# A causal mask moved from TensorE to GpSimd in the feed-forward attention of a four-layer kernel

## Reference, cut to what matters

```python
qkv = x @ W_qkv.T                                  # x is layer-normed
k_shared = einsum('bth,bthd->btd', indicator, k)   # one of 16 heads per token
v_shared = einsum('bth,bthd->btd', gating_top1, v)
att = einsum('bhqd,bkd->bhqk', q, k_shared) * (1.0 / sqrt(16))
att = where(tril, att, -inf)
att = softmax(att, axis=-1)
y = einsum('bhqk,bkd->bhqd', att, v_shared)
```

## Time and profile before

| | |
|---|---|
| time before, median of 3 runs | 1210.67 us (1209.03 to 1211.82) |
| the profiled execution: its time | 1211.78 us |
| the profiled execution: its span | 1210.0 us |
| busy: PE, PEld, DVE | 1032.8 us, 801.7 us, 755.6 us |
| busy: ACT, POOL | 523.2 us, 286.1 us |
| first feed-forward layer | about 344 us to 532 us |
| second feed-forward layer | about 1020 us to the end |

### The profile page before, as it was taken

The page is one execution under the profiler, slowest core; times in us unless marked ns, Lnnn a source line. Parts: engine busy times, 40 slices in busy tenths (PEclk is TensorE's granted clock), DMA queues, the critical chain, the costliest instruction groups (busy, mean ns, idle before and its releaser), DMA issues.

```text
span 1210.0 us, 20375 instructions
## 1 busy us (share of the span) xinstructions
PE 1032.8 (85%) x6976; PEld 801.7 (66%) x6976; DVE 755.6 (62%) x2242; ACT 523.2 (43%) x1369; POOL 286.1 (24%) x284
## 2 busy tenths in 40 slices
PE   0689999988758999946798989898998997799997
PEld 0577777776447777625676777676776776677764
DVE  5355666666358888713466656566565664788883
ACT  1114444344402444531256555455555564154545
POOL 4227667667700011000110101111010100000101
PEclk9867887778868999976899999899999998799999
DMA  4443322233023232241000000000000000433330
GB/s 174 71 71 72 68 56 63 59 57 61 1 44 76 59 77 59 47 152 62 1 2 1 2 2 1 1 1 1 1 1 1 1 1 2 87 77 76 85 77 29
DMA packets 56790, 53.71 MB, mean 44 GB/s; under 512 B 6240, under 2 KB 55408, under 8 KB 56560
## 3 DMA queue, kind: packets, MB, share of 16 engines
q1 hardware_dynamic: 56688, 52.41, 18.9%
HBM read 34.30 MB, written 17.30 MB: 43 GB/s over the span
## 4 chain that ended last, share of the span: by engine, by line
PE 69%; DVE 14%; POOL 8%; issue 4%; DMA 3%; ACT 2%; SPq 1%; POOLq 0%; ACTq 0%; DVEq 0%
PE bank L243 20%; PE bank L1529 6%; PE bank L1474 5%; PE bank L1332 4%; PE bank L1462 4%; PE bank L1537 3%; PE bank L1346 3%; PE bank L1329 3%; POOL weights L536 3%; PE bank L1515 2%; PE bank L1316 2%; PE bank L1367 2%; PE bank L348 1%; PE bank L1526 1%; DMA arena<-b_wo 1%
## 5 line engine op out<-in xcount | busy, mean ns | idle before, releaser
L972 DVE TENSOR_REDUCE arena<-bank 128x2 f32<-128x512 f32 (+1 forms) x192 | 129.7, 683 | 32.5 <-PE bank L1332 31.6
L670 ACT ACTIVATE weights<-bank 128x512 f32<-128x512 f32 x144 | 85.7, 596 | 109.1 <-PE bank L1346 108.9
L738 ACT ACTIVATE weights<-bank,neg_max 128x128 f32<-128x128 f32 (+1 forms) x256 | 105.0, 418 | 47.8 <-DVE neg_max L1123 47.7
L1332 PE MATMUL bank<-kf_stack,q_stack 96*128 96x128 f32 (+1 forms) x512 | 113.4, 327 | 0.0
L259 POOL TENSOR_SCALAR var_eps<-mv 128x2 f32<-128x2 f32 x32 | 7.0, 219 | 430.3 <-DVE mv L253 430.3
L536 POOL TENSOR_SCALAR weights<-weights 128x512 f32<-128x512 f32 x64 | 96.4, 1509 | 47.7 <-ACT weights L614 47.4
L1529 PE MATMUL bank<-kbT,arena 128*128 128x128 f32 (+1 forms) x512 | 107.1, 333 | 0.0
L1346 PE MATMUL bank<-q_stack,kf_stack 98*128 98x512 f32 x192 | 97.7, 513 | 0.0
L745 ACT ACTIVATE weights<-bank 128x384 f32<-128x384 f32 x128 | 62.7, 490 | 64.3 <-PE bank L1537 64.1
L1132 DVE TENSOR_SCALAR weights<-weights,inv_sum 128x128 f32<-128x128 f32 (+1 forms) x256 | 85.0, 374 | 4.5
L277 PE MATMUL bank<-cst,xn 128*128 128x128 f32 x128 | 24.0, 319 | 72.3 <-DVE xn L268 70.5
(11 more groups left out here) (214 smaller groups left out, 2724.8 us busy)
## 6 DMA issues: line engine op xcount, KB each, us to landing
q_stack<-scr_q SPq DMA_DIRECT2D x144, 128.0 KB, 3.7
scr_q<-q_hi SPq DMA_DIRECT2D x24, 256.0 KB, 2.3
scr_q<-q_lo SPq DMA_DIRECT2D x24, 256.0 KB, 2.5
ka_stack<-scr_k SPq DMA_DIRECT2D x48, 76.5 KB, 3.2
x_all<-x SPq DMA_DIRECT2D x8, 256.0 KB, 9.1
arena<-b_wqn SPq DMA_DIRECT2D x1, 2048.0 KB, 8.2
arena<-b_wo SPq DMA_DIRECT2D x1, 2048.0 KB, 17.0
out<-x_all SPq DMA_DIRECT2D x8, 256.0 KB, 2.3
```

The lines of the kernel that those rows point to most:

```text
L670: a.activation(pT[(STEPS * b + k) % N_PT], p2[k % 2][:, :], ACT.Exp).then_inc(s["exp"], 1)
L738: last = a.activation(probs[:, h % 4, t * P:t * P + n], ps_s[h % 2][:, t * P:t * P + n], ACT.Exp, bias=neg_max[:, h % 4, t:t + 1], accum_o ...
L972: v.tensor_reduce(into, p1[k % 2][:, :].rearrange("p (h k) -> p h k", h=n), AX.X, ALU.max, negate=True).then_inc(s["maxed"], 1)
L1332: last = mm(o[:, i, :], q_stack[b % 2][0:STK, h + i, t * P:(t + 1) * P], kf_stack[b % 3][0:STK, 0:(t + 1) * P], start=False, stop=i == n - ...
```

## The change

TensorE no longer writes a mask ahead of the second pass's scores. The scores matmul opens its bank itself, and ScalarE takes the exponential of all of them, later keys too. GpSimd then writes zero over the exponentials of later keys in the first 128 queries of each head of the item (two or four heads), in place in `pT`, where position decides: it keeps an element where query minus key (the partition) is at least zero. `attend_f` waits for this, by a new semaphore `causal`, in place of `exp`. On GpSimd's queue `causal(b-1, k)` stands behind `pool_rstd` at k = 3 and ahead of the residual at k = 8. The first pass keeps its mask.

```diff
+            zero = g.to_reg(0.0)
...
             def ffn(s):
+                def causal(b, k):
+                    n = 2 if k % 6 < 4 else 4
+                    part = pT[(STEPS * b + k) % N_PT].rearrange("p (h q) -> p h q", h=n)[:, :, 0:P]
+                    pool.wait_ge(*at(s, "exp", b, k + 1))
+                    g.affine_select(part, part, [[0, n], [1, P]], ALU.is_ge, zero, base=0, channel_multiplier=-1)\
+                        .then_inc(s["causal"], 1)
+
                 for b, k in steps_f():
                     if k == 3 and there(b + 2):
                         pool_rstd(s, b + 2)
+                    if there(b - 1):
+                        causal(b - 1, k)
                     if k == 8 and there(b - 2):
                         residual(s, b - 2, y_flat, at(s, "y", b - 2, 6))
...
-                def turned_mask(out_ap, n):
-                    mm(out_ap, mask_bf[:, :], ident_bf[:, :].unsqueeze(1).to_broadcast([P, n, P]), start=True, stop=False,
-                       skip_group_check=True)
...
                     pe.wait_ge(*at(s, "exp", b, k - 1))
-                    n, kb = (2, 0) if k % 6 < 4 else (4, 1)
-                    o = p2[k % 2][:, :].rearrange("p (h q) -> p h q", h=n)
-                    turned_mask(o[:, :, 0:P], n)
+                    kb = 0 if k % 6 < 4 else 1
                     mm(p2[k % 2][:, :], kf_stack[b % 3][:, kb * P:(kb + 1) * P], item_heads(q_stack[b % 2], k),
-                       start=False, stop=True, skip_group_check=True).then_inc(s["sT_ps"], 1)
+                       start=True, stop=True).then_inc(s["sT_ps"], 1)
...
-                    pe.wait_ge(*at(s, "exp", b, 6 * o + (6 if part == 2 else 4)))
+                    pe.wait_ge(*at(s, "causal", b, 6 * o + (6 if part == 2 else 4)))
```

More of the change, by code:

```diff
@@ L144, in hybrid_layers_kernel @@
         sf = [signals("ffn", "f", **TURNED, q_ps=1, kg_ps=2, k_sel=3, k48=3, kT_ps=1, k_stack=1, v_ps=1, v_sel=2,
-                      gate=11, gate_exp=1, s_ps=STEPS, maxed=STEPS, sT_ps=STEPS, exp=STEPS)]
+                      gate=11, gate_exp=1, s_ps=STEPS, maxed=STEPS, sT_ps=STEPS, exp=STEPS, causal=STEPS)]
         sf.append({**sf[0], "past": B})
```

## The result

The changed kernel takes 1203.41 us (median of 6 runs, 1200.88 to 1204.75) against 1210.93 us before (1209.03 to 1211.93): ratio 0.9939, 95% interval 0.9926 to 0.9952. 7.5 us are gained; 6.4 had been worked out from the profiled execution. The profiled execution after took 1204.43 us with a span of 1202.7 us.

What follows compares the result with a forecast made beforehand. TensorE was taken to bound steps 1 to 5 and slot 7, VectorE the stretch from step 6 to step 0. Per layer 7.3 - 4.1 = 3.2 us gained, 6.4 us for two, giving 1204 us; range 1190 to 1226.

Steps and rivals of the forecast that it cites:

- The price of the select: GpSimd's new operation, priced from L536: 0.82 us for 256 elements, 1.48 us for 512.
- The cheap rival: Selects up to about 1.0 us wide let GpSimd keep up in slots 7 and 8: 1191 us, chance 0.22.
- Its lower bound: Cheapest select price, from the MEMSET row's 0.86 ns an element: 0.30 us narrow, 0.52 us wide.
- The backlog in slots 7 and 8: GpSimd falls behind from item 4 of batch 6, then works 24.2 us without a pause to the last select.
- 2.8: Slots 7 and 8: masks removed gain 1.88 us and some 1.0 us, if nothing takes their place.
- A late tail: Layer's end: last attention and the copy, turn, quotients, residual and store behind it come 4.1 us later, after GpSimd's last select.
- The last sentence of the prediction: Prediction is wrong if select price or VectorE's stretch is misread, or TensorE, waiting in slot 8, falls to 1.2 GHz.
- Slots 1 to 6, 1.2 us each: Steps 1 to 5 gain 0.82 us, VectorE's stretch 0.4 us at most; 7.3 us for six slots.
- 0.4 us of slack: VectorE's stretch, step 6 to next step 0: x_lo is ready at 460.66, TensorE comes at 461.08; at most this is gained.
- VectorE is slowed by GpSimd: Two long SBUF reductions in VectorE's stretch slow down, 0.62 us a slot: 6.4 us gain eaten, 1212 us, chance 0.10.
- the dear price: Upper select price, 1.4 us narrow and 2.0 us wide: tail 16.5 us late, 1255 us; dear rival's chance 0.28.

Runs made afterwards that it cites:

- removal_only: Against the kernel before: second-pass masks removed, no select added, attention waits for the exponential; 1194.64 us, ratio 0.9857.
- late_residual: Changed kernel with each layer's last-but-one residual moved behind item 11's select of the last batch; 1202.53 us, ratio 0.9903 to the kernel before.
- mask_last: Changed kernel, but each layer's last batch keeps its TensorE mask and has no select; 1199.53 us, ratio 0.9889; run again 1201.63 us, 0.9924.
- decoy_select: Kernel before without second-pass masks; GpSimd does same-sized selects on a table nobody waits for, attention waits for the exponential; 1197.90 us, ratio 0.9892.
- res_early: Changed kernel with the last batch's mask kept on TensorE and the residual ahead of step 8's select; 1197.14 us, ratio 0.9900.
- norm_early: L268 moved ahead of step 5's maximum: on the changed kernel with last batch's TensorE mask kept 1201.92 us (0.9923); on the kernel before 1212.62 us (1.0011).
- both_early: Changed kernel with last batch's TensorE mask kept, L268 ahead of step 5's maximum, residual ahead of step 8's select; 1201.16 us, ratio 0.9915.
- changed_again: The changed kernel run a second time, unaltered, with another profile; 1204.60 us, ratio 0.9938 to the kernel before.
- select_only: Kernel before with masks kept on TensorE and the selects added, attention waiting for them; 1216.69 us, ratio 1.0039.

## Why the prediction was right, and where it wasn't

**The total.** 1204.0 us predicted, 1203.41 measured; 6.4 us of gain worked out, 7.5 measured. The second layer, from its first L268 to its last L500, takes 185.71 us before and 182.18 after, 3.5 us gained. By parts of that layer: up to the L356 at k = 1 of slot 2 it gains 1.04 us (55.17 to 54.13), from there to the L356 at k = 7 of slot 6 3.38 us (94.23 to 90.85), from there to the last L314 1.49 us (25.20 to 23.71), and the tail takes 2.38. The sum is 3.5 us. I had 7.3 - 4.1 = 3.2. (By the prediction's own terms the last select ends at 1183.0 + 24.2 = 1207.2, which makes the tail 4.0 us late, and halfway between 1204 and 1255 is 1230 and not 1225; neither slip matters.)

**The price of the select: wrong.** 0.82 and 1.48 us were taken from L536; it is 0.41 and 0.65. The cheap rival had the price right and its result wrong: it said 1191 us. Its lower bound, 0.30 and 0.52 us, carried a base of 0.08 us that none of its rows gives; with the 0.16 us that I had worked out from L529 it would have been 0.38 and 0.60. I had given weight to likeness in operands and place; the slope was close to that of the MEMSET, which reads nothing. The rule of the Trainium skill that I cited beside it, "GPSIMD Engine Reference", section "Performance pitfalls for Q7 kernels" (a compare-select body not unrolled, 2.03 cycles an element), gives an estimate of 1.0 us for the wide one, and the measured 0.65 is below it as well. The same passage of the Trainium skill has 1.03 cycles for that body unrolled twice, which I left aside; at the 1.2 GHz of its page that is an estimate of 0.86 ns an element, and the measured 0.94 is near it.

**The backlog in slots 7 and 8: wrong.** "From there to the last select [...] without a pause" did not happen. GpSimd is busy 6.76 of 13 us and 8.26 of 19 us there. Slots 7 and 8 give 1.5 us, where I had 2.8 less a backlog. Without any select (removal_only) they give 1.9 (25.20 to 23.29), so the 2.8 were too much by themselves.

**A late tail: right in effect, wrong in cause and size.** I had all of it behind GpSimd, by 4.1 us; it is 2.4 us, 0.2 from one residual in front of three selects, 0.66 from the select's own latency and, for the largest part, 1.6 from a fall of the clock. The last sentence of the prediction named that fall as what could go wrong, with no price. late_residual and mask_last show the first two, the pair of executions of the unchanged code shows the third.

**Slots 1 to 6, 1.2 us each: the term was mis-sized, for two reasons.** The 0.82 us of steps 1 to 5 are right: from k = 1 to k = 7 a slot gains 0.82 us (11.91 to 11.09), with selects and without. In VectorE's stretch the 0.4 us of slack were 0.18 (removal_only, 8.68 to 8.50). Then the selects' load takes 0.35 us back, all of it there (8.50 to 8.85). decoy_select shows that it is the load and not a wait, and res_early that it sits in L1024 (193 to 306 ns) and L1036 (159 to 375 ns), together 0.33 us. Of that 0.23 came back there, and the rest, 0.11 us, had moved on to the instruction behind L1036 (192 to 304 ns).

**The rival "VectorE is slowed by GpSimd": true, and argued through the wrong instructions.** I looked at the long reductions, because they are long, and found them no candidates; they are not (1.05 and 1.03 us). But in the same stretch stand L1024 with two SBUF inputs and L1036 from SBUF to SBUF, which I had not priced because they are short. The rule of the Trainium skill that I had cited ("GPSIMD Engine Reference", section "Specifications": VectorE instructions with two SBUF inputs or in a two-port mode contend with GpSimd) agrees with L1024 by its operands. What mode L1036 and L268 run in no trace shows, so whether the rule covers them stays open. That L268 itself costs nothing, as I had said, norm_early confirms. The rival's effect is 5 x 0.35 us a layer, some 3.5 us for both.

**How two errors made a right total.** It was luck. In the second layer, slots 1 to 6 up to their last L356 gave 2.9 us less than forecast (1.04 + 3.38 = 4.4 against 7.3), and what follows lost 0.9 us (2.4 - 1.5) in place of 4.1, 3.2 us better. The two misses come from different terms, and the second depends on the clock: where it was kept, the tail was 1.6 us shorter. So the agreement of the totals confirms neither term.

**A better version.** mask_last_res_early leaves the last batch's mask on TensorE and puts the residual ahead of step 8's select: 1197.14 us, ratio 0.9900 (0.9872 to 0.9929), with a span of 1195.9 us in its profile. By its slot and its tail it is, with both_early, the best of those that mask every batch: 0.23 us x 10 slots and 2.4 us x 2 tails under the changed kernel, 7 us. Beside changed_again it measured 7.5 us less by the medians and 4.6 by the ratios. Its lead over mask_last alone, 1199.53 and 1201.63 us, is shown by the slot's and the second layer's length (178.73 against 179.98 and 179.87 us) and not by the intervals of the ratios, which overlap.

## What to carry to other kernels

Work moved to GpSimd is paid for on VectorE. Before pricing the move, list the VectorE instructions of the critical stretch that take their input from SBUF alone, the short ones too, and ask which of them the new work will lie over; where a neighbour in the queue can be shifted so that they don't meet, much of the price comes back (0.23 of 0.35 us a slot here); look at what they meet then, since the collision may only move on.

A pipeline's last batch is another kernel than its middle. Where nothing covers a latency any more, keep the old path there, and put what nobody waits for (the residual here) behind what TensorE waits for: its 1.3 us in front of three awaited selects cost the layer 0.2 us where the clock held behind the wait, and 1.8 where it fell.

For an operation that no row shows, work the sum through with each neighbouring row's price before choosing one. The sum of the tail was worked through with the middle and the dear price only; worked through with the MEMSET's, it has no backlog, and what is left to ask is what still stands in front of the awaited selects.

## What was not expected of the hardware

- The affine select costs 0.94 ns an element over some 0.17 us, about a third of the 2.59 ns of `tensor_scalar` with max in place (L536) on the same buffers.
- A short VectorE instruction that begins under a GpSimd one can last until that one ends. In select_only the gate's product of 128x32 elements takes 515 ns on average, where 193 is usual:

```profile
454.41 0.17 DVE L1022 TENSOR_REDUCE arena<-arena 128x2 f32<-128x32 f32 x1
454.62 0.17 DVE L1023 RECIPROCAL arena<-arena 128x2 f32<-128x2 f32 x1
454.82 0.52 DVE L1024 TENSOR_TENSOR arena<-arena 128x32 f32<-128x32 f32 x1
```

  The residual lies over all three (454.01 to 455.29 in that trace), and the product ends 0.05 us after it. The reduction and the reciprocal beside it, with one input, take their usual 0.17 us. In mask_last_res_early an instruction that began 0.04 us ahead of the select kept its 0.16 us.
- The granted clock fell behind a wait of TensorE of 1.17 us in one execution and not behind one of 1.18 us in another of the same code. The fall cost 1.6 us.
